# Graph attention layer on one core: the first two node tiles take relu before the deviation is known, and GpSimd takes more of the norm steps

## What is computed

```python
h = jnp.maximum(_layernorm(x, axis=-1), 0.0)
# inside the layer, x is h and adj_a = adj_b = adj
type_sum = adj @ x
attn_a = sigmoid(concat([type_sum, x], 1) @ Wa.T + ba)      # attn_b with Wb, bb
h = x @ W_sa
scores = (h @ a_sa[0, :Hd])[:, None] + (h @ a_sa[0, Hd:])[None, :]
e = jnp.where(adj_a != 0, jnp.exp(-leaky_relu(scores, 0.01)), 0.0)
x_a = (e / (e.sum(1, keepdims=True) + 1e-05)) @ h
x_b = adj @ (x @ W_gcnb) + b_gcnb
out = x_in + sigmoid(attn_a * x_a + attn_b * x_b)
```

## Time and profile before

| | us |
|---|---|
| median of 3 runs | 177.54 |
| lowest, highest | 177.13, 178.27 |
| the profiled execution, its own time | 176.94 |
| its span in the trace | 175.1 |
| PE busy | 170.5 |
| granted TensorE clock, mean of the span | 0.997 |

### The profile page before, as it was taken

The page is one execution under the profiler, slowest core; times in us unless marked ns, Lnnn a source line. Parts: engine busy times, 40 slices in busy tenths (PEclk is TensorE's granted clock), DMA queues, the critical chain, the costliest instruction groups (busy, mean ns, idle before and its releaser), DMA issues.

```text
span 175.1 us, 3378 instructions
## 1 busy us (share of the span) xinstructions
PE 170.5 (97%) x1313; PEld 124.6 (71%) x1313; DVE 144.5 (83%) x306; ACT 113.2 (65%) x167; POOL 24.5 (14%) x43
## 2 busy tenths in 40 slices
PE   7999999999999999999999999999999999999992
PEld 2556764455554478888744488888888888888892
DVE  3799995589999995999999703999999999976551
ACT  3769996349868889298658600875875874863310
POOL 4846441002007930000000000000000000000000
PEclk9999999999999999999999999999999999999998
DMA  5999999986999369900010100000010010011101
GB/s 135 296 213 260 226 231 175 207 157 110 215 220 332 146 112 216 247 28 2 0 64 0 60 0 0 4 0 0 4 60 0 6 60 0 4 62 60 64 30 30
DMA packets 9071, 17.66 MB, mean 101 GB/s; under 512 B 3920, under 2 KB 4704, under 8 KB 8288
## 3 DMA queue, kind: packets, MB, share of 16 engines
q0 software_dynamic: 1728, 8.39, 25.0%
q1 hardware_dynamic: 7328, 9.06, 16.3%
HBM read 22.94 MB, written 2.11 MB: 143 GB/s over the span
## 4 chain that ended last, share of the span: by engine, by line
PE 97%; DVE 1%; issue 0%; ACT 0%; DVEq 0%
PE ps L822 32%; PE ps L865 16%; PE ps L863 16%; PE ps L864 16%; PE ps L856 6%; PE ps L797 6%; PE ps L905 3%; PE ps L791 1%; PE ps L926 0%; DVE logit L771 0%; DVE e_lo L557 0%; PE ps L818 0%; ACT logit L434 0%; DVE res L664 0%; DVE e_hi L519 0%
## 5 line engine op out<-in xcount | busy, mean ns | idle before, releaser
L863 PE MATMUL ps<-mv_lo,e_hi 128*128 128x257 f16 (+2 forms) x272 | 71.0, 267 | 0.0
L865 PE MATMUL ps<-mv_hi,e_lo 128*128 128x257 f16 (+2 forms) x272 | 70.9, 266 | 0.0
L864 PE MATMUL ps<-mv_hi,e_hi 128*128 128x257 f16 (+2 forms) x272 | 70.8, 266 | 0.0
L400 ACT ACTIVATE z<-z,log_e 128x1024 f32<-128x1024 f32 x32 | 36.7, 1146 | 31.2 <-DVE z L601 31.2
L601 DVE SCALAR_TENSOR_TENSOR z<-sl_row,exs,far 128x512 f32<-128x512 f32 x64 | 45.1, 746 | 0.6 <-DMA sl_row<-sl_line 0.6
L609 DVE TENSOR_TENSOR e_lo<-z,e_hi 128x1024 f16<-128x1024 f32 x32 | 39.0, 1220 | 1.4 <-ACT e_hi L410 1.4
L822 PE MATMUL ps<-adj,nat_lo 128*128 128x512 f16 x128 | 36.8, 379 | 0.0
L822 PE MATMUL ps<-adj,nat_hi 128*128 128x512 f16 x128 | 36.7, 379 | 0.0
L410 ACT ACTIVATE e_hi<-z 128x1024 f16<-128x1024 f32 x32 | 33.3, 1041 | 0.0
L863 PEld LDWEIGHTS ps<-mv_lo,e_hi 128*128 128x128 f16 x272 | 26.4, 97 | 3.4 <-ACT c_sb L388 0.3
L864 PEld LDWEIGHTS ps<-mv_hi,e_hi 128*128 128x128 f16 x272 | 26.5, 98 | 3.1
(11 more groups left out here) (69 smaller groups left out, 170.0 us busy)
## 6 DMA issues: line engine op xcount, KB each, us to landing
adj<-in_adj_t POOLq DMA_DIRECT2D x6, 1024.0 KB, 9.8
x_sb<-in_x SPq DMA_DIRECT2D x6, 512.0 KB, 8.2
out<-res SPq DMA_DIRECT2D x7, 256.0 KB, 2.0
adj<-in_adj_t POOLq DMA_DIRECT2D x4, 256.0 KB, 6.7
adj<-in_adj_t POOLq DMA_DIRECT2D x2, 512.0 KB, 8.7
x_sb<-in_x SPq DMA_DIRECT2D x3, 256.0 KB, 4.0
sl_row<-sl_line SPq DMA_DIRECT2D x2, 256.0 KB, 5.5
sl_row<-sl_line SPq DMA_DIRECT2D x1, 512.0 KB, 7.0
```

What stands on the lines that cost most here:

```text
L400: act.activation(z[:, n % ZRING, :, :], z[:, n % ZRING, :, :], ACT.Exp, bias=log_e[:, 0:1], scale=SLOPE - 1.0).then_inc(exp_done, 1)
L863: pe.matmul(ps[:, bank, cols], e_hi[:, s, i1], mv_lo[:, j, cols], start=(j == 0), stop=False)
L864: pe.matmul(ps[:, bank, cols], e_hi[:, s, i1], mv_hi[:, j, cols], start=False, stop=False)
L865: return pe.matmul(ps[:, bank, cols], e_lo[:, s, i1], mv_hi[:, j, cols], start=False, stop=(j == NT - 1))
```

## The change

Tiles 0 and 1: ACT takes relu of x minus mean as soon as the mean is known, without the deviation, which is positive and can be applied afterwards. DVE scales the identity by 1/deviation (`diagonal`, stored in the still unused `res`), and PE's transposing product (`turn_scaled`) multiplies by that matrix, as an ordinary float32 product where before it was a transpose. The untransposed parts get 1/deviation in `first_nat_highs` and `first_nat_lows`. One warm-up product is dropped.

The high part of the wide weights goes from DVE to ACT (`w_wide_high`). PE's products of tile 1 wait for the low part of the tile only at their third pair. From unit 3 on POOL computes `var_s` and `neg_mean` (`POOL_FROM`). In POOL's queue the adjacency piece of tiles 6 and 7 goes behind unit 3's steps, and that of tiles 8 to 11 behind unit 4's.

```diff
+POOL_FROM = 3
+NCENTRED = 2
...
+        diag = res[:, 0, :, 0:P]
...
             def norms(u):
                 ts = slice(*UNITS[u])
-                pool.wait_ge(var_ready, u + 1)
+                if u < POOL_FROM:
+                    pool.wait_ge(var_ready, u + 1)
+                else:
+                    pool.wait_ge(moments_done, UNITS[u][1])
+                    pool.tensor_scalar(var_s[:, ts], mean_var[:, ts, 1], LN_EPS, H_SCALE ** -2, ALU.add, ALU.mult).then_inc(var_ready, 1)
+                    pool.tensor_scalar(neg_mean[:, ts], mean_var[:, ts, 0], -1.0, None, ALU.mult).then_inc(neg_ready, 1)
+                    pool.wait_ge(var_ready, u + 1)
                 pool.tensor_tensor(rstd[:, ts], var_s[:, ts], power[:, 0:UNITS[u][1] - UNITS[u][0]], ALU.pow).then_inc(rstd_ready, 1)
+                if u < NCENTRED:
+                    return
...
             norms(2)
             load_adj(2)
+            norms(3)
             load_adj(3)
-            norms(3)
+            norms(4)
             load_adj(4)
-            norms(4)
             load_adj(5)
...
+            def centred(u):
+                act.wait_ge(centre_ready, u + 1)
+                act.activation(x_sb[:, u, :], x_sb[:, u, :], ACT.Relu, bias=neg_mean[:, u:u + 1], scale=1.0).then_inc(h0_done, 1)
...
+            def first_nat_highs():
+                act.wait_ge(rstd_ready, NCENTRED)
+                for t in range(NCENTRED):
+                    ins = act.activation(nat_hi[:, t, :], x_sb[:, t, :], ACT.Copy, scale=rstd[:, t:t + 1])
+                ins.then_inc(nat_high, 1)
+
+            def w_wide_high():
+                act.wait_ge(wa_landed, 16)
+                act.activation(wa_hi[:, :, 0:WG], wa_sb[:, :, :], ACT.Copy, scale=W_SCALE).then_inc(wa_high, 1)
...
                 for t in range(lo, hi):
                     dve.bn_stats(stats[:, t, :], x_sb[:, t, :]).then_inc(stats_done, 1)
+                    if t == NCENTRED:
+                        diagonal(1)
...
+            def diagonal(u):
+                if u == 0:
+                    dve.wait_ge(ident_ready, 3)
+                dve.wait_ge(rstd_ready, u + 1)
+                dve.tensor_scalar(diag[:, u, :], ident[:, :], rstd[:, u:u + 1], None, ALU.mult).then_inc(diag_ready, 1)
+
+            def w_wide_low():
...
+            def turn_scaled(u):
+                pe.wait_ge(diag_ready, u + 1)
+                pe.wait_ge(h0_done, u + 1)
+                for k in range(KT):
+                    ins = pe.matmul(turn_bank(u)[:, 0, k, :], x_sb[:, u, k * P:(k + 1) * P], diag[:, u, :], start=True, stop=True)
+                ins.then_inc(turned, 1)
...
-            pe.wait_ge(var_ready, 1)
+            pe.wait_ge(centre_ready, 1)
             warm(2)
-            pe.wait_ge(norm_ready, 1)
+            turn_scaled(0)
             warm(1)
-            pe.wait_ge(ident_ready, 3)
-            turn(0)
-            warm(1)
-            turn(1)
+            turn_scaled(1)
...
-            wide(1)
+            pe.wait_ge(wa_ready, 1)
+            pe.wait_ge(h0t_high, 2)
+            wide_part(1, slice(0, WA), ((0, 0), (0, 1)))
+            pe.wait_ge(h0t_ready, 2)
+            wide_part(1, slice(0, WA), ((1, 0),)).then_inc(wide_product, 1)
             wide_part(0, slice(WG, WA)).then_inc(wide_product, 1)
```

More of the change, by code:

```diff
@@ L168, in build @@
         var_ready = sem("var_ready")
+        centre_ready = sem("centre_ready")
+        diag_ready = sem("diag_ready")
         rstd_ready = sem("rstd_ready")
         norm_ready = sem("norm_ready")
+        neg_ready = sem("neg_ready")
         h0_done = sem("h0_done")
@@ L308, in norms @@
                 ts = slice(*UNITS[u])
-                pool.wait_ge(var_ready, u + 1)
+                if u < POOL_FROM:
[5 more added lines that the diff above has]
+                    pool.wait_ge(var_ready, u + 1)
                 pool.tensor_tensor(rstd[:, ts], var_s[:, ts], power[:, 0:UNITS[u][1] - UNITS[u][0]], ALU.pow).then_inc(rstd_ready, 1)
+                if u < NCENTRED:
+                    return
                 pool.wait_ge(rstd_ready, u + 1)
+                if u >= POOL_FROM:
+                    pool.wait_ge(neg_ready, u + 1 - POOL_FROM)
+                if u < POOL_FROM:
+                    pool.wait_ge(centre_ready, u + 1)
                 pool.tensor_tensor(shift[:, ts], neg_mean[:, ts], rstd[:, ts], ALU.mult).then_inc(norm_ready, 1)
@@ L359, in _ @@
         def _(act):
+            def centred(u):
+                act.wait_ge(centre_ready, u + 1)
+                act.activation(x_sb[:, u, :], x_sb[:, u, :], ACT.Relu, bias=neg_mean[:, u:u + 1], scale=1.0).then_inc(h0_done, 1)
             def h0_tiles(u):
-                act.wait_ge(norm_ready, u + 1)
+                act.wait_ge(norm_ready, u + 1 - NCENTRED)
                 for t in range(*UNITS[u]):
@@ L437, in _ @@
             act.activation(table[:, :], log_e[:, :], ACT.Exp)
-            h0_tiles(0)
-            h0_tiles(1)
+            centred(0)
+            centred(1)
             h0t_highs(0)
+            w_wide_high()
             h0t_highs(1)
+            first_nat_highs()
             h0_tiles(2)
-            nat_highs(0)
             nat_highs(1)
@@ L530, in moments @@
                     dve.bn_aggr(mean_var[:, t, :], stats[:, t, :]).then_inc(moments_done, 1)
[L531 to L538, removed]
+                if u < POOL_FROM:
+                    dve.wait_ge(moments_done, hi)
+                    dve.tensor_scalar(var_s[:, lo:hi], mean_var[:, lo:hi, 1], LN_EPS, H_SCALE ** -2, ALU.add, ALU.mult)\
+                        .then_inc(var_ready, 1)
+                    dve.tensor_scalar(neg_mean[:, lo:hi], mean_var[:, lo:hi, 0], -1.0, None, ALU.mult).then_inc(centre_ready, 1)
+            def diagonal(u):
[4 more added lines that the diff above has]
+            def w_wide_low():
                 dve.wait_ge(wa_high, 1)
@@ L557, in h0t_lows, with first_nat_lows @@
                 dve.tensor_tensor(h0t_tiles(h0t_lo, u), turn_bank(u), h0t_tiles(h0t_hi, u), ALU.subtract).then_inc(h0t_ready, 1)
+            def first_nat_lows():
+                dve.wait_ge(nat_high, 1)
+                for t in range(NCENTRED):
+                    ins = dve.scalar_tensor_tensor(out=nat_lo[:, t, :], in0=x_sb[:, t, :], scalar=rstd[:, t:t + 1],
+                                                   in1=nat_hi[:, t, :], op0=ALU.mult, op1=ALU.subtract)
+                ins.then_inc(nat_ready, 1)
             def nat_lows(p):
@@ L672, in _ @@
             moments(1)
+            diagonal(0)
             moments(2)
-            w_wide()
             h0t_lows(0)
+            w_wide_low()
             w_scores()
@@ L678, in _ @@
             moments(3)
-            nat_lows(0)
+            first_nat_lows()
             narrow_results(0)
@@ L805, in wide @@
                     pe.wait_ge(h0t_landed[u - NTURN], 32)
-                if u == 1:
-                    pe.wait_ge(wa_ready, 1)
                 for t in range(*UNITS[u]):
```

## The result

After the change the kernel takes 178.88 us, median of 6 runs (178.50 to 180.12), beside 177.31 us before (6 runs, 176.59 to 178.27). The ratio is 1.0101, with a 95% interval of 1.0058 to 1.0144: slower by 1%, and above the range forecast.

What follows compares the result with a forecast made beforehand. PE bounds the kernel: the time is when its gapless stream of adjacency products starts (10.47 us), plus the stream. Terms -0.42 +0.43 +0.50 -0.33 = +0.2 us gave a median of 177.7 us, range 177.0 to 178.7.

Steps and rivals of the forecast that it cites:

- PE's queue starts the first product: First transpose of tile 0: PE's warm-up products, not the data, set its start; 5.42 instead of 5.84, gain 0.42 us.
- Fp32 products, +0.43: Tile 0's transposes as full fp32 products: four instructions at 0.215 us instead of two, 0.86 instead of 0.43 us.
- first rival: Head: fp32 products are cheap (0.12 us each) or the clock rises earlier, so the earlier relu pays; 177.0 to 177.4; chance 0.22.
- second rival: Head: fp32 products are dear, 0.43 us each at the lower pace, delaying everything behind by 1.0; 178.5; chance 0.10.
- Weights on ScalarE, +0.50: Wide weights' high part, behind tile 0's copy on ScalarE, ends at 7.5; PE's first real product at 7.55 instead of 7.04.
- Tile 1 does not wait for its low part, -0.33: Tile 1's first four products on PE no longer wait for its low part, which gives back 0.33 us.
- Diagonal, cover of GpSimd's steps: Diagonal scaling takes 0.15 to 0.42 us; GpSimd's added steps delay unit 3's shift 0.6 to 0.7, cover 0.8, costing nothing.
- No row here separates that effect: Unit 3's power on GpSimd, 1.09 us beside a DVE subtraction: the trace cannot show whether the two exclude each other.
- third rival: From unit 3 on: GpSimd's two added ops take 0.7 to 2.6 us each, PE stands at tiles 4 and 5; 177.9 to 181.7; chance 0.10.
- Adjacency of tiles 6 and 7, hidden: Piece issued at 12.1 instead of about 8 us lands near 18, before PE wants it at 19.31; no cost.
- fourth rival: The late adjacency piece holds PE at 19.3 for up to 2 us; 178.2 to 179.7; chance 0.08.
- Same within 1%: Whole kernel: a measurement tells about 1% (1.8 us) from no change; chance 0.05 slower, 0.03 faster than that.

Runs made afterwards that it cites:

- the head alone: Changed kernel with DVE computing variances and GpSimd's transfers in their old places, leaving the new treatment of tiles 0 and 1 and weights split: 177.49 us, ratio 0.9990.
- transposes-first kernel: Changed kernel with the first transfer-made transposes (tiles 10 and 11) put ahead of the score line's spread in SP's queue: median 184.48 us, no ratio given.

## Why the prediction was wrong

The forecast was 177.7 us with 1.0 us above it in the range; it came out at 178.88. Step by step:

**PE's queue starts the first product.** Right for this execution, to the hundredth: 5.42. It holds while the zeros run at the lower pace. In four profiles in which the clock rises before they end, the first product comes at 4.97 to 5.39.

**Fp32 products, +0.43.** The price was right and the clock was not. Four took 5.42 to 5.91, 0.12 us each on average, my lower bound, so the term is +0.06 beside the two transposes of before (0.43) instead of +0.43. But the product of zeros behind them has a duration of 0.38 us (0.63 in the same place of before), so the clock rose to its higher level of 2.4 GHz within the first of them. The kernel with only tiles 6 and 7 late shows the lower level:

```profile
5.42 0.84 PE L849 MATMUL ps<-res,x_sb 128*128 128x128 f32 x4
6.09 0.38 PE L961 MATMUL ps<-e_hi 128*128 128x512 f16 x1
```

Its four start at 5.42, 5.63, 5.84 and 5.98: 0.21 us each until the clock rises, the 0.215 of the sum. So the first rival won by its second condition, the earlier rise, and not by its first, and the second rival (0.43 each) is refuted.

**Weights on ScalarE, +0.50.** About right as a length (0.63 us measured for 0.625) but all of it 0.4 to 0.5 earlier, since the copy of tile 0 came at 6.11 instead of 6.52. PE's wide product stood at 7.07 instead of 7.55. Net against before, this link costs nearly nothing here (7.04). In eight of the other profiles PE does stand 0.3 to 0.5 us for it, as the prediction had it.

**Tile 1 does not wait for its low part, -0.33.** Right: its first product runs at 8.71, 0.3 ahead of the 9.00 of before, and its three groups of products follow without a gap. In all the head gained 0.3 us where the sum said +0.2.

**Diagonal, cover of GpSimd's steps.** Right. The scaling took 0.27 to 0.29 us, inside 0.15 to 0.42. Variance, minus mean, power and shift of unit 3 took 0.32, 0.36, 1.20 and 0.20 us, ScalarE started at 12.19, and PE turned the tiles at 13.46 without a gap. That 12.2 was forecast is partly luck: the two steps took 0.3 us more than reckoned and the power 0.1 more, while the statistics, forecast half a microsecond later, were done near 9.85, as before. The run with GpSimd's steps kept and only the order undone says it by time, 0.9996. At unit 3 the added steps took more than the 0.2 us each that I had from the shift, 0.32 and 0.36, where DVE ran `nat_lo` steps from 9.77 on; at unit 4 they took 0.18 and 0.24. The power shows the same more clearly. At unit 3 it starts while DVE subtracts for `nat_lo` (10.61 to 11.29), at unit 4 while DVE runs no such step:

```profile
10.68 1.20 POOL L325 TENSOR_TENSOR rstd<-var_s,power 128x2 f32<-128x2 f32 x1
...
13.33 0.72 POOL L325 TENSOR_TENSOR rstd<-var_s,power 128x2 f32<-128x2 f32 x1
```

In every profile here, from unit 3 on, a power of two tiles takes 0.69 to 0.72 us where it starts ahead of such a step or away from it, and 0.95 to 1.27 where it starts during one or together with it; the variance step, 0.18 to 0.20 in the other units behind unit 3, takes 0.54 in the last one, beside such a step. The prediction's "No row here separates that effect" was thus wrong. The Trainium skill ("SBUF — State Buffer", section "SBUF: two separate sides") says that GpSimd and a DVE instruction with two SBUF inputs exclude each other and that the one which starts first has the port; these rows agree with it, though no run isolates it. By size it was 0.1 to 0.6 us an instruction and stayed inside the cover. The prediction priced that case at 178.1, where its own third rival has 177.9 for 0.7 us each.

**Adjacency of tiles 6 and 7, hidden.** This is the step that failed. What it says of the piece itself held: issued at 12.10, landed 4.9 us later at 17.0 (earlier than any case of the sum), where PE wants it at about 19. I wrote "what is not moved for this piece is moved for x, and the queue ahead has shrunk", and stopped at that. Both halves are true, and together they are the fault: x is then finished early, and from 15 to 19 us SP's queue brings nothing beside GpSimd's. I followed the piece to its own reader and not the rest of the two queues to theirs. All of it was in the trace of before: a store that takes 6.7 us, a spread and transposes behind it in SP's queue, and a transpose that landed 1.6 us ahead of its use. That margin was the number to look up. The sum had nothing for this piece; the order of the pieces measures 1.0089 by itself, 1.6 us.

My fourth rival had the right cause (late pieces) and the right size (178.2 to 179.7), but the wrong reader: it put the wait at 19.3 and was dismissed because that reader had cover. The price is shown by both directions: the order alone costs 0.89%, undoing it gives the whole loss back, half of it costs about half. The links in between (store, spread, transposes) are read from the traces and not isolated. Of the two kernels that moved them, one shortened the store to 4.9 us and made what stands behind it late; the other issued the transposes at 26.2 and 27.7, and the second landed at 45.7. In the changed kernel's profile the links end at tile 10, with the new order alone at chunk 2.

**Same within 1%.** With 0.05 for slower and 0.03 for faster the rest, 0.92, stood on this. The measured ratio is on the border, 1.0101 with an interval that spans it. A chance of 0.05 for the other side was too small, as it came from two rivals at named places and left no room for a reader that I hadn't looked for.

**Where the head's gain went.** The stream starts 0.3 us earlier in the profile of the changed kernel. Over the ten profiles with the new head it starts at 9.62 to 10.28, mean 9.99, and in the three with the old one and all its zeros at 10.22 to 10.40, mean 10.31, so 0.3 us is the mean gain and a single execution can miss it. Yet the head alone has a ratio of 0.9990 (0.9969 to 1.0012), which would hide a gain of 0.3 us (0.17%) as well as none. What the profiles show is that two waits stand right behind it: the first piece of chunk 2, for which PE waits 0.3 and 0.5 us near 49.5 in two of the kernels with the old order, and ScalarE's copy of the score line near 63 us. No version here beats the kernel before by more than the measurement tells.

Open: why the transpose takes 8.3 us in the changed kernel (6.7 before, 5.7 with the new order alone), contention with the next chunk's pieces or its place in SP's queue; the spread of the runs of the transposes-first kernel.

## What to carry to other kernels

When a transfer is issued later, its own reader is the smallest part of the question. Look at the stretch that it leaves and at what moves instead: here another queue finished early and fell idle, the bytes missed were not made up, and what was issued afterwards on both queues landed later. Then follow each queue to every reader with little margin; here a 2 KB store and the transposes behind it, 20 us after the edit, and behind these the first piece of chunk 2.

A gain at the head is worth no more than the slack to the next wait, so find the next two waits before counting it. And take its size from several profiles: here one execution's stream starts up to 0.4 us beside the mean.

## What the runs showed of the hardware

The time of a small transfer is set by what surrounds it: the same 2 KB store took 4.9, 6.7, 8.7 and 9.4 us in four kernels, and 14.7 in the 189.27 us execution of a fifth. The Trainium skill, "DMA: Bandwidth & Descriptors", section "Issuing engines are not separate DMA queues", says that transfers of all issuing engines run and interleave on the same 16 transfer engines; the traces agree, since SP's store grew from 6.7 to 9.4 us when only GpSimd's issues were moved. More surprising is that a large load of SP's, issued while GpSimd's queue is full, brings next to nothing for 3 to 4 us: two packets from 15.45 to 19 us for wg_sb issued at 15.45, and one from 19 to 23 us for the same load issued at 19.42 in the kernel before. Whether it is SP's queue having fallen idle or what GpSimd's has in line no run separates. For the second speaks that x's last load of the kernel before, issued at 10.72 right behind the others, moved 20 packets from 12 to 14 us and 93 from 14 to 16, and that wg_sb issued at 25.52, when GpSimd's pieces of the first chunk had landed, moved 47 packets within the microsecond from 26 on.

The moment at which TensorE reaches its higher clock is not the same in executions that begin alike, with products of zeros every 0.42 us: in the profile of before the pace rises near 6.9 us, in the kernel before with only ScalarE's later copy moved the two transposes take 0.22 us together from 5.83, in the changed kernel it rises within the first product from 5.42, and in the kernel with one warm-up product less near 4.1. Part of the spread in the start of the stream (9.62 to 10.40) goes with it. The row of granted clock reads 9 in all of these slices, so in the head the durations have to be read instead.
